# Adding two rope products on VectorE instead of GpSimd, with one of them in the projection's bank, and loading the attention result behind most of the last transposes

## The chip, the cores and the metric

The kernel runs on one core of a Trainium2 chip. The metric is device time in microseconds (us) of one execution. The median of three runs before the change is 1959.97 us.

## What is computed

One transformer layer over 2048 tokens of width 512, in float32: layer norm, RMS norm with a weight, attention with 32 query heads in 8 groups (4 query heads share one key and one value head of 64), rotary embedding of queries and keys, causal softmax, output projection and residual; then layer norm and a feed-forward part with ternary weights.

```python
y = rms_norm(layernorm(x)) * rms_w
y = einsum('bsm,cm->bsc', y, w_in)            # q: 32*64, k: 8*64, v: 8*64
q, k = rope(q), rope(k)                       # x1*cos - x2*sin, x2*cos + x1*sin
attn = softmax(where(causal, q @ k.T / 8, -inf))
x = x + layernorm(x) + (attn @ v) @ w_out.T
x = x + down(silu(up(layernorm(x))) * gate(layernorm(x)))
```

## The kernel before

Every product is kept at more than 16 bits by splitting a number into a high and a low half: high*high, high*low and low*high are added up in PSUM. Three blocks follow one another: `normalise`, `attention` and `output_projection` with the feed-forward part. The change lies in `attention`.

`attention` runs over 8 groups. A group has 16 units, one for each of 4 chunks of 512 queries and each of 4 heads, and a unit goes over the keys up to its chunk in tiles of 128: in all 160 steps, numbered through the group. In a step TensorE makes the scores of one key tile for 512 queries (L598, L599, and L602 on the diagonal), ScalarE takes the exponential (L666), GpSimd subtracts the high half from it, which leaves the low half `pl` (L827, "low part"), and five steps later TensorE multiplies exponentials and values (L615 to L619, "the values of a step"). Those wait for the exponential and for the low part.

Beside the steps runs side work, placed by hand in two tables of step numbers. `JOB_STEPS` gives the steps at which TensorE projects a tile of 128 tokens for the chunks to come (`project`, L567, 12 matmuls): in a middle group steps 0, 4, 10, 16, 26, 27, 42, 53, 88, 101, 118, 123, 141, 146, 151 and 155. `GANG_STEPS` gives the steps at which it makes four score tiles whose maximum per query is wanted (`max_gang`, L583, in two pairs); VectorE reduces them (L742, L746). Projections and these score tiles take turns in four PSUM banks. The bank that an item takes must have been read by the fourth item before it: `side_read` waits for that. For a projection it waits for `v_low`, which the last of four VectorE instructions raises. The gang that follows a projection takes the projection's bank for its fourth tile, in the second pair.

A projected tile goes through `out_of_bank` on VectorE (v's high half, product with the cosines, product of the turned halves with the sines, v's low half). GpSimd adds the two products (`rope_sum`, L833), ScalarE makes high halves of queries and keys (L677 to L680, `qk_high_part`, five steps behind the projection), GpSimd their low halves (L842, `qk_low_part`). The SP queue then turns them by DMA transposes, in the order of the table `TRANSFERS`: q_hh (L448) is wanted by the first gang of a unit, the keys (L465) too, q_lm (L457) by the unit's first scores. The same table turns (L477) and stores (L487) each chunk's result. Every engine executes in program order, so a wait holds up all that stands behind it there.

The opening projects eight tiles before the first group. The last group has no projections ahead (steps 88 to 155 are free of them). In it `load_result` puts four DMAs of 512 KB (L495) into the SP queue, which bring the first two result tiles for the output projection.

Of the kernel before, what the change touches and what calls it, by code (L numbers as in the profile page):

```python
# [11 lines left out]
ALU = mybir.AluOpType  # L12
# [7 lines left out]
TT = S // P  # L20
DH = 64
GROUPS = 8
HG = 4
# [6 lines left out]
NCH = S // CHUNK  # L30
# [186 lines left out]
SUM_LAG = 2  # L217
HI_LAG = 5
QK_LOW_LAG = 4
TILES_KEPT = 4  # L220
# [4 lines left out]
def step_of(i):  # L225
    u = max(w for w in range(UNITS) if FIRST_STEP[w] <= i)
    return u, i - FIRST_STEP[u]
# [121 lines left out]
def slot(part, n):  # L349
    return part[n] if 0 <= n < len(part) else (None, None, [])  # L350
# [7 lines left out]
def attention(nc, w_in_t, w_out_t, attn_dram, yh, yl, consts, cos, sin, wraw, wh, wl, wscale, raw, z_out, late, att_in):  # L358
# [6 lines left out]
    with ExitStack() as ctx:  # L365
        sb = lambda name, shape, dt: ctx.enter_context(nc.sbuf_tensor(name, shape, dt))
        sem = lambda name: ctx.enter_context(nc.semaphore(name))
        ident16, big, mask_kq, mask_qk = (consts[:, i, :] for i in range(4))
        rope_a = sb("rope_a", [P, TILES_KEPT, HG + 1, DH], F32)
        rope_b = sb("rope_b", [P, TILES_KEPT, HG + 1, DH], F32)  # L370
# [4 lines left out]
        v = sb("v", [P, 2, TT, VW], F16)  # L375
# [23 lines left out]
        w_high = sem("w_high")  # L399
        w_low = sem("w_low")  # L400
        misc_ready = sem("misc_ready")
        rope_parts = sem("rope_parts")
        v_high = sem("v_high")
        v_low = sem("v_low")
        roped_ready = sem("roped_ready")
        qk_high = sem("qk_high")
        qk_low = sem("qk_low")
# [30 lines left out]
        def _(sp):  # L438
# [74 lines left out]
            for g in range(GROUPS):  # L513
                final = g == GROUPS - 1
                if not final:
                    sp.wait_ge(w_low, (g + 1) * KT)
                    load_w(g + 1)
                if g == 1:
                    sp.wait_ge(z_out, 16 * NCH)
                sp.wait_ge(exp_done, g * STEPS + EXP_AHEAD)  # L520
                for kind, c, *arg in TRANSFERS:
                    if final and arg[1] == 1:
                        continue
                    {"turn": turn_out, "store": store, "hh": query_high, "lm": query_low, "k": keys}[kind](g, c, *arg)
                    if kind == "store" and 1 <= g <= CT // NCH:
                        load_w_out((g - 1) * NCH + c)
                    if kind == "store" and final and c == 1:
                        load_result()
            sp.wait_ge(w_loaded, 16 * GROUPS)
            sp.wait_ge(w_out_in, 16 * CT)  # L530
# [9 lines left out]
        def _(pe):  # L540
            pe.wait_ge(ones_set, 2)
            def group(g, par, part):
                def side_read(kind, ahead, *arg):

                    if kind == "piece":
                        pe.wait_ge(maxs_used, (g + ahead) * PIECES + FIRST_STEP[arg[0]] + arg[1] + 1)
                    else:
                        pe.wait_ge(v_low, (g + ahead) * TT + arg[0] + 1)

                def take_bank(*item):  # L550

# [168 lines left out]
        def _(dve):  # L720
# [8 lines left out]
            def group(g, par, part):  # L729
# [27 lines left out]
                def out_of_bank(ahead, t):  # L757
                    gg, side, b = g + ahead, par ^ ahead, t % TILES_KEPT
                    bank = side_bank(part, ("proj", ahead, t))
                    halves = bank[:, 0:ROPED].rearrange("p (h a d) -> p h a d", h=HG + 1, a=2)  # L760
                    by_half = lambda a: a.rearrange("p (a d) -> p a d", a=2).unsqueeze(1).broadcast_to([P, HG + 1, 2, DH // 2])
                    roped = lambda a: a[:, b].rearrange("p h (a d) -> p h a d", a=2)
                    dve.wait_ge(misc_ready, gg * TT + t + 1)
                    dve.wait_ge(qk_low, gg * TT + t + 1)
                    nc.vector.tensor_scalar(v[:, side, t, 0:DH], bank[:, ROPED:GC], 1.0 / W_SCALE, None,
                                            ALU.mult).then_inc(v_high, 1)
                    nc.vector.tensor_tensor(roped(rope_a), halves, by_half(cos[:, t, :]), ALU.mult)
                    nc.vector.tensor_tensor(roped(rope_b), halves[:, :, ::-1, :], by_half(sin[:, t, :]), ALU.mult)\
                        .then_inc(rope_parts, 1)
                    dve.wait_ge(v_high, gg * TT + t + 1)  # L770
                    nc.vector.scalar_tensor_tensor(v[:, side, t, VL:VW], bank[:, ROPED:GC], 1.0 / W_SCALE,
                                                   v[:, side, t, 0:DH], ALU.mult, ALU.subtract).then_inc(v_low, 1)

                def unit_out(u):
                    by_tile = obank(u).rearrange("p (t w) -> p t w", w=VU)
# [38 lines left out]
        @block.gpsimd  # L814
        def _(pool):

            nc.gpsimd.memset(qk_lo[:, :, 0:HG, :, 1, :], 0.0).then_inc(rows_set, 1)
            nc.gpsimd.memset(qk_hi[:, :, HG, :, 1, 1:DH], 0.0).then_inc(rows_set, 1)
            nc.gpsimd.memset(qk_hi[:, :, HG, :, 1, 0:1], -1.0).then_inc(rows_set, 1)
            pool.wait_ge(ones_set, 2)  # L820
            def group(g, par, part):
                def low_part(i, ahead=0):
                    u, j = step_of(i)
                    r = first_query_tile(u // HG, j)
                    cols = slice(r * P, CHUNK)
                    pool.wait_ge(exp_done, (g + ahead) * STEPS + i + 1 + EXP_AHEAD)
                    nc.gpsimd.tensor_tensor(pl[:, i % RING, cols], p32[:, i % RING, cols], p_high[:, i % RING, cols],  # L827
                                            ALU.subtract).then_inc(low_ready, 1)

                def rope_sum(ahead, t):  # L830
                    b = t % TILES_KEPT
                    pool.wait_ge(rope_parts, (g + ahead) * TT + t + 1)
                    nc.gpsimd.tensor_tensor(rope_a[:, b], rope_a[:, b], rope_b[:, b], ALU.add).then_inc(roped_ready, 1)  # L833

                def qk_low_part(ahead, t):
                    (c, tt), gg = divmod(t, TPC), g + ahead
                    pool.wait_ge(qk_high, gg * TT + t + 1)
                    if tt == 0 and (ahead or c >= 2):
                        for h in range(HG):
                            pool.wait_ge(lm_in[c % 2][h], 16 * (2 * gg + c // 2))  # L840
                        pool.wait_ge(k_in[(c - 2) % NCH], 32 * (gg + (c >= 2)))
                    nc.gpsimd.tensor_tensor(qk_lo[:, c % 2, :, tt, 0, :], rope_a[:, t % TILES_KEPT], qk_hi[:, c % 2, :, tt, 0, :],  # L842
                                            ALU.subtract).then_inc(qk_low, 1)

                for n in range(len(part) + 2):
                    step = slot(part, n - 1)[0]
                    if step is not None:
                        if step >= HEAD:
                            low_part(step)
                    if job := slot(part, n - QK_LOW_LAG)[1]:  # L850
                        qk_low_part(*job[1:])
                    if job := slot(part, n - SUM_LAG)[1]:
                        rope_sum(*job[1:])
                for i in range(HEAD if part in (OPENING, SLOTS) else 0):
                    low_part(i, ahead=int(part is SLOTS))

            group(0, 0, OPENING)
            every_group(group)
# [507 lines left out]
```

## Time and profile before

| what | value |
|---|---|
| runs, median of 3 (lowest to highest) | 1959.97 us (1959.13 to 1960.13) |
| profiled execution, its own time | 1961.57 us |
| its span | 1959.8 us |
| TensorE busy | 1894.3 us (97%) |
| GpSimd busy | 1421.3 us (73%) |
| VectorE busy | 1220.8 us (62%) |
| ScalarE busy | 932.3 us (48%) |
| attention stage | about 43 to 1444 us of the span |

Busy time is the time in which at least one instruction of the engine ran. Matmuls are pipelined and their ends are modelled, so consecutive ones overlap in the record; what TensorE does is read from the distance between starts. Numbers in the text such as 600.77 are microseconds from the start of the span.

### The profile page before, as it was taken

The numbers are of one execution on the slowest core, as the hardware profiler recorded it, in microseconds if no ns is written. First come the engines' busy times: TensorE is split into PE (matmuls) and PEld (weight loads), VectorE is DVE, ScalarE is ACT, GpSimd is POOL, SyncE is SP. The second block draws the span as 40 slices with busy tenths as digits, with TensorE's granted clock in tenths as the row PEclk, the third lists the DMA queues.
The fourth block names the chain that finished last, engine by engine and source line by source line (L and its number), as shares of the span: only waits on it lengthen the run. The fifth ranks groups of instructions, "written<-read, shape, count | busy, mean of one in ns | idle before, by whom it ended". The sixth has DMA issues, their size and how long they took to land. (4 is left out here: it accounts for less than half of the span.)

```text
span 1959.8 us, 55709 instructions
## 1 busy us (share of the span) xinstructions
PE 1894.3 (97%) x21382; PEld 1093.0 (56%) x21382; DVE 1220.8 (62%) x3283; ACT 932.3 (48%) x1997; POOL 1421.3 (73%) x1627
## 2 busy tenths in 40 slices
PE   4899999999999999999999999998999999999999
PEld 3565666666566666556656665665644444444444
DVE  7787588668758866875886687585726563131221
ACT  4465656556565665655566565555722212120110
POOL 2799989999998999999899999988940002131221
PEclk7999999999999999999999999999999999999999
DMA  6343242333225224332422332144146520000000
GB/s 213 67 68 56 49 97 56 50 83 74 64 50 99 56 47 85 70 69 48 91 50 40 79 63 62 32 90 88 38 154 226 203 86 1 22 0 21 5 16 22
DMA packets 301814, 136.82 MB, mean 70 GB/s; under 512 B 248576, under 2 KB 285696, under 8 KB 300032
## 3 DMA queue, kind: packets, MB, share of 16 engines
q1 hardware_dynamic: 301568, 133.43, 29.7%
q8 instruction: 168, 2.75, 0.6%
q14 instruction: 78, 0.64, 0.1%
HBM read 49.48 MB, written 25.17 MB: 38 GB/s over the span
## 5 line engine op out<-in xcount | busy, mean ns | idle before, releaser
L827 POOL TENSOR_TENSOR pl<-p 128x512 f16<-128x512 f32 (+3 forms) x1280 | 1135.9, 920 | 44.6 <-ACT p L666 44.0
L666 ACT ACTIVATE p<-a_ps 128x512 f32<-128x512 f32 (+3 forms) x1280 | 672.9, 532 | 515.2 <-PE a_ps L599 329.0
L742 DVE TENSOR_REDUCE mpart<-a_ps 128x1 f32<-128x512 f32 x768 | 485.2, 684 | 156.1 <-PE a_ps L583 153.9
L615 PE MATMUL a_ps<-v,p 128*128 128x65 f16 x4352 | 530.4, 194 | 10.9 <-POOL pl L827 5.7
L617 PE MATMUL a_ps<-v,p 128*128 128x64 f16 x4352 | 529.5, 194 | 0.0
L615 PEld LDWEIGHTS a_ps<-v,p 128*128 128x128 bf16 x4352 | 407.2, 97 | 218.5 <-issue 89.3
L619 PE MATMUL a_ps<-v,pl 128*128 128x65 f16 x4352 | 526.2, 192 | 0.0
L599 PE MATMUL a_ps<-q_lm,k_h 128*128 128x512 f16 (+3 forms) x1280 | 445.0, 348 | 0.0
L598 PE MATMUL a_ps<-q_hh,k_hl 128*128 128x512 f16 (+3 forms) x1280 | 444.2, 347 | 0.0
L617 PEld LDWEIGHTS a_ps<-v,p 128*128 128x128 bf16 x4352 | 406.7, 98 | 64.1 <-issue 0.3
L619 PEld LDWEIGHTS a_ps<-v,pl 128*128 128x128 f16 x4352 | 407.6, 99 | 0.0
L746 DVE CUSTOM_DVE_ANT_0 masked<-a_ps,causal 128x128 bf16<-128x128 f32 (+3 forms) x512 | 228.4, 485 | 45.4 <-PE a_ps L583 45.3
L991 POOL TENSOR_TENSOR yl<-o_turn_late,yh 128x512 f16<-128x512 f32 x64 | 74.3, 1163 | 231.1 <-DVE yh L962 231.1
L902 PE MATMUL p_ps<-xh,tern 128*128 (+1 forms) x512 | 194.0, 379 | 0.0
L902 PE MATMUL p_ps<-xl,tern 128*128 (+1 forms) x512 | 194.0, 379 | 0.0
L583 PE MATMUL a_ps<-k_h,q_hh 64*128 64x512 f16 (+2 forms) x640 | 173.0, 339 | 16.5 <-DMA q_hh<-qk_hi 7.9
L583 PE MATMUL a_ps<-k_hl,q_hh 64*128 64x512 f16 (+1 forms) x640 | 187.7, 362 | 0.0
L567 PE MATMUL a_ps<-wh,yh 128*128 128x384 f16 x512 | 168.5, 329 | 8.3 <-DVE v L725 6.8
L567 PE MATMUL a_ps<-wl,yh 128*128 128x384 f16 x512 | 168.1, 328 | 0.0
L567 PE MATMUL a_ps<-wh,yl 128*128 128x384 f16 x512 | 168.1, 328 | 0.0
L942 ACT ACTIVATE p_below<-p_ps,tern_scale 128x512 f32<-128x512 f32 x64 | 43.9, 687 | 249.7 <-PE p_ps L902 249.7
L1130 PE MATMUL p_ps<-yl,yh 128*128 128x512 f16 x480 | 145.6, 379 | 0.0
(103 smaller groups left out, 2373.1 us busy)
## 6 DMA issues: line engine op xcount, KB each, us to landing
yh<-attn_scratch SPq DMA_DIRECT2D x32, 512.0 KB, 4.3
raw<-ffn_t SPq DMA_DIRECT2D x12, 1024.0 KB, 5.0
attn_scratch<-o_turn SPq DMA_DIRECT2D x32, 256.0 KB, 3.1
attn_scratch<-o_turn_late SPq DMA_DIRECT2D x32, 256.0 KB, 2.8
wraw<-w_in_t SPq DMA_DIRECT2D x8, 768.0 KB, 4.8
resid_scratch<-raw SPq DMA_DIRECT2D x4, 1024.0 KB, 4.5
raw<-w_out_t SPq DMA_DIRECT2D x16, 256.0 KB, 3.5
x<-resid_scratch SPq DMA_DIRECT2D x4, 1024.0 KB, 7.8
```

The lines of the kernel that those rows point to most:

```text
L567: last = nc.tensor.matmul(bank[:, 0:GC], a[:, kt, tok], b[:, kt, :], start=(kt == 0 and n == 0), stop=(kt == KT - 1 and n == 2))
L583: nc.tensor.matmul(banks[n % 2][:, 0:width], q_hh[rows, c % 2, h, t * P:(t + 1) * P], keys[rows, par ^ ahead, kk * CHUNK:kk * CHUNK + widt ...
L598: nc.tensor.matmul(out, k_hl[:, side, keys], q_hh[:, c % 2, h, r * P:CHUNK], start=True, stop=False)
L599: last = nc.tensor.matmul(out, k_h1[:, side, keys], q_lm[:, c % 2, h, r * P:CHUNK], start=False, stop=not diag)
L615: nc.tensor.matmul(o, weights, v[:, par, j, 0:VU], start=(j == 0 and t == 0), stop=False, skip_group_check=True)
L617: nc.tensor.matmul(o[:, 0:DH], weights, v[:, par, j, VL:VW], start=False, stop=False, skip_group_check=True)
L619: last = nc.tensor.matmul(o, pl[:, i % RING, t * P:(t + 1) * P], v[:, par, j, 0:VU], start=False, stop=(j == TPC * c + t), skip_group_chec ...
L666: nc.scalar.activation(p32[:, i % RING, r * P:CHUNK], sbank(i)[:, r * P:CHUNK], ACT.Exp, scale=SCALE).then_inc(exp_done, 1)
L742: nc.vector.reduce_max(mpart[:, u % 2, t, kk:kk + 1], bank, AX.X).then_inc(maxs_used, 1)
L746: nc.vector.tensor_tensor_reduce(masked[:, n % 2, 0:width], bank, causal[:, CHUNK - width:CHUNK], 1.0, -LEAST, ALU.add, ALU.max, mpart[:, ...
L827: nc.gpsimd.tensor_tensor(pl[:, i % RING, cols], p32[:, i % RING, cols], p_high[:, i % RING, cols], ALU.subtract).then_inc(low_ready, 1)
L902: last = nc.tensor.matmul(bank, w[:, k, e * P:(e + 1) * P], x[:, k, bass.ds(c * CHUNK, CHUNK)], start=(k == 0 and x is xh), stop=(k == KT ...
```

## The change

The add of the two rope products moves from GpSimd to VectorE. So that VectorE reads one operand from PSUM, the product with the cosines is written over the projection in its bank, after the turned product has been read out of it; the new semaphore `rope_turned` keeps these two apart. The semaphore `v_low` goes, and the bank is now released by `roped_ready`, raised by the add. `load_result` moves in the order of the last group's transfers from behind the store of chunk 1 to behind the q_lm of chunk 3, head 2 (unit 14).

```diff
-                    if kind == "store" and final and c == 1:
+                    if final and (kind, c, arg[0]) == ("lm", NCH - 1, HG - 2):
                         load_result()
...
-                        pe.wait_ge(v_low, (g + ahead) * TT + arg[0] + 1)
+                        pe.wait_ge(roped_ready, (g + ahead) * TT + arg[0] + 1)
...
                     nc.vector.tensor_scalar(v[:, side, t, 0:DH], bank[:, ROPED:GC], 1.0 / W_SCALE, None,
                                             ALU.mult).then_inc(v_high, 1)
-                    nc.vector.tensor_tensor(roped(rope_a), halves, by_half(cos[:, t, :]), ALU.mult)
                     nc.vector.tensor_tensor(roped(rope_b), halves[:, :, ::-1, :], by_half(sin[:, t, :]), ALU.mult)\
-                        .then_inc(rope_parts, 1)
+                        .then_inc(rope_turned, 1)
+                    dve.wait_ge(rope_turned, gg * TT + t + 1)
+                    nc.vector.tensor_tensor(halves, halves, by_half(cos[:, t, :]), ALU.mult).then_inc(rope_parts, 1)
                     dve.wait_ge(v_high, gg * TT + t + 1)
                     nc.vector.scalar_tensor_tensor(v[:, side, t, VL:VW], bank[:, ROPED:GC], 1.0 / W_SCALE,
-                                                   v[:, side, t, 0:DH], ALU.mult, ALU.subtract).then_inc(v_low, 1)
+                                                   v[:, side, t, 0:DH], ALU.mult, ALU.subtract)
+                    dve.wait_ge(rope_parts, gg * TT + t + 1)
+                    nc.vector.tensor_tensor(roped(rope_a), halves, roped(rope_b), ALU.add).then_inc(roped_ready, 1)
...
-                def rope_sum(ahead, t):
-                    b = t % TILES_KEPT
-                    pool.wait_ge(rope_parts, (g + ahead) * TT + t + 1)
-                    nc.gpsimd.tensor_tensor(rope_a[:, b], rope_a[:, b], rope_b[:, b], ALU.add).then_inc(roped_ready, 1)
-
...
-                    if job := slot(part, n - SUM_LAG)[1]:
-                        rope_sum(*job[1:])
```

VectorE's rows for one tile of a middle group, before (the bank is `a_ps`):

```order
L765 TENSOR_SCALAR v<-a_ps 128x64 [waits qk_low,misc_ready]
L767 TENSOR_TENSOR rope_a<-a_ps,cos_sb 128x320
L768 TENSOR_TENSOR rope_b<-a_ps,sin_sb 128x320
L771 SCALAR_TENSOR_TENSOR v<-a_ps,v 128x64 [waits v_high]
L742 TENSOR_REDUCE mpart<-a_ps 128x1 [waits maxs_ready] x2
```

And at the same place of the change:

```order
L765 TENSOR_SCALAR v<-a_ps 128x64 [waits qk_low,misc_ready]
L767 TENSOR_TENSOR rope_b<-a_ps,sin_sb 128x320
L770 TENSOR_TENSOR a_ps<-a_ps,cos_sb 128x320 [waits rope_turned]
L772 SCALAR_TENSOR_TENSOR v<-a_ps,v 128x64 [waits v_high]
L775 TENSOR_TENSOR rope_a<-a_ps,rope_b 128x320 [waits rope_parts]
```

The products have changed places, a wait on VectorE's own result stands before each of the last two operations that need one, and the add follows v's low half.

The SP queue in the last group, behind the store of chunk 1 (- before, + the change):

```order
+L448 DMA_TRANSPOSE q_hh<-qk_hi 128x4x128
+L457 DMA_TRANSPOSE q_lm<-qk_lo 128x4x128
+L448 DMA_TRANSPOSE q_hh<-qk_hi 128x4x128
+L457 DMA_TRANSPOSE q_lm<-qk_lo 128x4x128
+L448 DMA_TRANSPOSE q_hh<-qk_hi 128x4x128
+L457 DMA_TRANSPOSE q_lm<-qk_lo 128x4x128
+L477 DMA_TRANSPOSE o_turn<-o_hl 128x8x128 x2
+L487 DMA attn_scratch<-o_turn 128x4x256 x2
+L448 DMA_TRANSPOSE q_hh<-qk_hi 128x4x128
+L457 DMA_TRANSPOSE q_lm<-qk_lo 128x4x128
 L495 DMA yh<-attn_scratch 128x2048 x4
```

The load (L495) now has ten more entries of the queue ahead of it; one q_lm, that of the last unit, stays behind it.

## Rows read from the trace of the kernel before

**Rows 1.** Windows: one middle group; busy us and instructions of each engine, clock, DMA.

```profile
587.60:759.60 172.00, 170.12 (x2368) 105.36 (x2368) 126.20 (x356) 102.40 (x229) 166.19 (x193) 1.00 0.35 68
```

**Rows 2.** Groups by line and shape, count | busy us, mean ns | idle before.

```profile
L833 POOL TENSOR_TENSOR rope_a<-rope_a,rope_b 128x320 f32<-128x320 f32 x128 | 110.8, 866 | 16.8 <-DVE rope_b L768 16.8
...
L768 DVE TENSOR_TENSOR rope_b<-a_ps,sin_sb 128x320 f32<-128x320 f32 x114 | 54.9, 481 | 0.0
...
L779 DVE TENSOR_TENSOR a_ps<-a_ps,rden 128x256 f32<-128x256 f32 x123 | 53.2, 433 | 4.2
...
L732 DVE SCALAR_TENSOR_TENSOR wl<-wraw,wscale,wh 128x384 f16<-128x384 f32 x28 | 32.5, 1161 | 0.0
...
L787 DVE TENSOR_TENSOR o_hl<-a_ps,o_hl 128x256 f16<-128x256 f32 x60 | 25.0, 416 | 2.0 <-ACT o_hl L695 2.0
```

**Rows 3.** Timeline of VectorE, tile of step 10: start us, us, instruction.

```profile
598.77 0.17 DVE L777 RECIPROCAL rden<-a_ps 128x4 f32<-128x4 f32 x1
598.98 0.43 DVE L779 TENSOR_TENSOR a_ps<-a_ps,rden 128x256 f32<-128x256 f32 x1
599.48 0.22 DVE L765 TENSOR_SCALAR v<-a_ps 128x64 f16<-128x64 f32 x1
599.62 0.48 DVE L767 TENSOR_TENSOR rope_a<-a_ps,cos_sb 128x320 f32<-128x320 f32 x1
600.02 0.48 DVE L768 TENSOR_TENSOR rope_b<-a_ps,sin_sb 128x320 f32<-128x320 f32 x1
600.41 0.21 DVE L771 SCALAR_TENSOR_TENSOR v<-a_ps,v 128x64 f16<-128x64 f32 x1
```

**Rows 4.** Timeline of TensorE, second pair of step 12: [idle before <-releaser].

```profile
600.77 0.21 PE L583 MATMUL a_ps<-k_h,q_hh 64*128 64x128 f16 x1 [0.18 <-DVE v L771]
```

**Rows 5.** Timelines of VectorE and TensorE, tile of step 88.

```profile
682.04 0.21 DVE L771 SCALAR_TENSOR_TENSOR v<-a_ps,v 128x64 f16<-128x64 f32 x1
...
682.45 0.38 PE L583 MATMUL a_ps<-k_h,q_hh 64*128 64x512 f16 x1
```

**Rows 6.** Timeline of TensorE at a group's end.

```profile
757.74 0.22 PE L602 MATMUL a_ps<-consts 128*128 128x128 f16 x1
758.14 0.19 PE L615 MATMUL a_ps<-v,p 128*128 128x65 f16 x1 [0.18 <-POOL pl L827]
...
759.19 0.22 PE L602 MATMUL a_ps<-consts 128*128 128x128 f16 x1
759.82 0.19 PE L615 MATMUL a_ps<-v,p 128*128 128x65 f16 x1 [0.41 <-POOL pl L827]
```

**Rows 7.** Timeline of GpSimd at the same end.

```profile
756.34 0.86 POOL L833 TENSOR_TENSOR rope_a<-rope_a,rope_b 128x320 f32<-128x320 f32 x1
```

**Rows 8.** Timelines of ScalarE and GpSimd behind the tile of step 53.

```profile
651.74 0.24 ACT L680 ACTIVATE qk_lo<-rope_a 128x64 f16<-128x64 f32 x1
...
652.25 0.80 POOL L842 TENSOR_TENSOR qk_lo<-rope_a,qk_hi 128x320 f16<-128x320 f32 x1
```

**Rows 9.** Last group: timelines of SP, TensorE, GpSimd; windows; landing times of L448.

```profile
1354.90 1.68 SPq L448 DMA_TRANSPOSE q_hh<-qk_hi  x1
...
1402.98 19.77 SPq L457 DMA_TRANSPOSE q_lm<-qk_lo  x2
...
1363.53 0.61 PE L583 MATMUL a_ps<-k_h,q_hh 64*128 64x512 f16 x1 [6.77 <-DMA q_hh<-qk_hi]
...
1349.38 11.75 POOL L827 TENSOR_TENSOR pl<-p 128x512 f16<-128x512 f32 x13
...
1373.71 68.62 POOL L827 TENSOR_TENSOR pl<-p 128x512 f16<-128x512 f32 x75 [0.40 <-ACT p L666]
...
1364.00:1366.00 2.00, 2.00 (x19) 0.95 (x16) 1.82 (x4) 0.00 (x0) 0.00 (x0) 0.50 0.00 0
...
DMA to landing us min/median/max: 2.4/2.5/8.6
```

More of the change, by code:

```diff
@@ L401, in attention @@
         misc_ready = sem("misc_ready")
+        rope_turned = sem("rope_turned")
         rope_parts = sem("rope_parts")
         v_high = sem("v_high")
-        v_low = sem("v_low")
         roped_ready = sem("roped_ready")
```

## The prediction

> **What bounds the kernel now.** I take the windows of one middle group first [rows 1]. In 172.0 us TensorE is busy 170.1, GpSimd 166.2, VectorE 126.2 and ScalarE 102.4. Two engines look full. GpSimd's 166 us are honest: its operations follow one another. TensorE's are too many, since a matmul's shown end lies behind the start of the next, so what TensorE really waits for has to be read from the distance of starts. Seven groups of this kind and a shorter last one make the attention stage, so a tenth of a microsecond at one step of a group is worth 0.7 to 0.8 us.
>
> Next come the operations of the change by shape [rows 2]: the rope add costs GpSimd 0.866 us (0.82 from its start to the next one's, since neighbours overlap a little). VectorE's product over 320 columns takes 0.481, one over 256 columns from PSUM to PSUM 0.433 and from PSUM to SBUF 0.416.
>
> Then the timeline of VectorE at one token tile, the third of the group (step 10) [rows 3], and of TensorE behind it [rows 4]. VectorE begins at 599.48 and ends with v's low half at 600.41 + 0.21 = 600.62. The four scoring matmuls of step 12 come next on TensorE. Their second pair, which takes the projection's bank, starts at 600.77, released by that very instruction. So here the bank's release is already what TensorE waits for, and 0.15 us pass from VectorE's end to the matmul.
>
> Last, two places where GpSimd holds TensorE up. At the group's end the values of steps 157 and 159 start 0.40 and 0.63 us behind the matmul before them, where 0.05 to 0.06 is usual (a 128-column matmul at 2.4 GHz): 0.34 + 0.57 = 0.9 us of standstill, both released by GpSimd [rows 6]. And in the last group TensorE stands 6.77 us for a transpose of queries [rows 9].
>
> **The change, part by part.**
>
> *VectorE.* Five instructions in place of four. From the start of v's high half to the bank's release it is now 600.62 - 599.48 = 1.14 us. In the new order the turned product starts at 0.14 and ends at 0.62. The product with the cosines waits for it. Such a wait on the engine's own result is in the trace: the reciprocal ends at 598.77 + 0.17 = 598.94 and the instruction that waits for it starts at 598.98, 0.04 later [rows 3]; without a wait the next starts 0.08 before the end. So the product starts at 0.66 instead of 0.54. It writes into PSUM, which costs 0.01 to 0.02 more over 256 columns [rows 2]; v's low half follows at 1.07, and the add at 1.20, when the product has been ready since 1.16. The add over 320 columns, one operand in PSUM, is like the product (0.48): end at 1.68. The bank is released 0.53 us later, and VectorE is occupied 0.53 us longer (0.40 for the add, 0.12 for the broken overlap, 0.01 for PSUM). Call it x. Neither end is certain, for no in-place product over 320 columns and no such add is in the trace: below, x = 0.41 if the own wait costs nothing (add and PSUM alone); above, 0.65, if both own waits cost what the first does. I take 0.53, by the rows of the same shapes.
>
> The Trainium skill, "VectorE: DVE Perf Modes", section Terms, says that a flush is emitted after every VectorE operation and the next can't issue until the pipe is empty. By that rule operations never overlap, the wait on rope_turned costs nothing, x would be 0.41 and the sum below 1957.5 us. The trace does not show it so: rope_b starts 0.08 us before rope_a ends [rows 3].
>
> Where does x reach TensorE? At steps 4, 10 and 16 the gang of four two slots later has its second pair waiting for the bank, and VectorE has next to no idle time between; three times 0.53 = 1.6 us. That VectorE is pushed as far behind does not add to it, for TensorE comes as late. At step 88 TensorE takes the bank at 682.45, v's low half having ended at 682.04 + 0.21 = 682.25 [rows 5]: of 0.53 only 0.05 is hidden, 0.5 us. At the tiles of steps 27, 42, 53, 101 and 146 the bank is taken 0.3 to 0.6 us after its release, less the 0.15 that passes anyhow; there 0.05 to 0.2 each comes through, 0.6 together (my estimate, in the manner of rows 5). The other six have over 0.8 us. Loss of a group: 1.6 + 0.5 + 0.6 = 2.7 us.
>
> *GpSimd.* 16 adds of 0.82 us go from each group, 13 us of its 166. They count only where TensorE stands for GpSimd. At the group's end GpSimd's chain is the add at 756.34 [rows 7], the low parts of steps 157 and 158, the part qk_lo of the tile, and the low part of step 159. Without this add and the one at step 153, the low parts of 157 and 159 come some 1.5 us earlier, more than the 0.34 and 0.57 us that TensorE stands: all 0.9 us is gained. (The part qk_lo reads a copy by ScalarE that waits for the same add, and moves up with it.) Behind the tiles of steps 26 and 27 a standstill of 0.2 us goes. The third place is steps 65 to 78, where GpSimd runs without a pause since step 55 and TensorE loses 1.3 us. There an add and the 0.82 us of it go, but the part qk_lo that follows at 652.25 reads what ScalarE writes until 651.74 + 0.24 = 651.98, and ScalarE's place for it is between the exponentials of steps 57 and 58 [rows 8]. So GpSimd would reach it 0.6 to 0.8 us early and wait: 0.2 is left, and this tile's gang comes 0.26 later through VectorE. I count nothing. Gain of a group: 0.9 + 0.2 = 1.1 us.
>
> Net: 2.7 - 1.1 = 1.6 us lost in each of seven groups, 11.2 us. The last group has no tiles at steps 88 to 155 and ends behind GpSimd anyway: 1.6 + 0.4 - 0.2 = 1.8 us lost. The opening has nothing of the end of a group; what it loses (its first pieces take the last tile's bank) stands in place of group 0's step 4.
>
> *The load.* Four transfers of 512 KB leave the SP queue ahead of q_hh for unit 12. That transpose was issued at 1354.90, and TensorE resumed at 1363.53: it is the slowest of the line, 8.6 us to land where 2.5 is the median [rows 9]. Moved behind the q_lm of unit 14, the load passes four q_hh, four q_lm, the turn and the store of chunk 2. The stall of 6.77 us goes, and the granted clock of 0.50 (1.2 GHz) that follows it with it. But TensorE is not what ends this group: from 1373.71 GpSimd works 68.62 us without a pause, to the stage's last values. Before that it stood from 1349.38 + 11.75 = 1361.13 on, save for steps 79 to 84, six low parts (three of 512 columns, one each of 384, 256 and 128) that are 4.7 us of work back to back. It can start these at 1361.1, so it ends 1373.71 - 1361.13 - 4.7 = 7.9 us earlier; TensorE is then ahead of it by some 2 us and stays so. The last two q_lm, issued at 1402.98 and 18.6 us later [rows 9], move up with it: the load is issued near 1396 and there some 9 us after (as q_hh was, queued behind it), 30 us ahead of its use and 8 ahead of the last q_lm. Gain 7.9 us; bounds 7.0 (if part of TensorE's lead is lost) and 9.0 (if TensorE's whole loss counted: 6.8, and half of some 5 us at the lower clock).
>
> **Sum.** 11.2 + 1.8 - 7.9 = 5.1 us more. The profiled execution took 1961.57 us (span 1959.8 and 1.8 around it) and is 1.6 above the median of 1959.97; it would be 1966.7, and the median **1965.1 us**.
>
> **Rivals.**
> - *VectorE's part is cheaper* (x of 0.40 to 0.47). For: 57 us of result hang on each microsecond of x, and the own wait rests on one kind of row. At x = 0.41 a group loses 1.7 - 1.1 = 0.6 us: 4.2 + 1.2 - 7.9 = -2.5, 1957.5 us.
> - *GpSimd's relief is worth all it seems to be.* For: it is 97% busy. If steps 65 to 78 also give 0.8 us, a group loses 0.8: 5.6 + 1.0 - 7.9 = -1.3, 1958.7 us. Against: ScalarE's place in rows 8.
> - *The bank's later release reaches TensorE nowhere* (faster). If x stays under 0.36, so that little comes through at steps 4 to 16, the result passes below -3.9; were it wholly hidden, each group would gain 1.1: -7.7 - 0.2 - 7.9 = -15.8, 1944 us. Against: the release named in rows 4.
> - *The add collides with GpSimd.* wl<-wraw, which reads SBUF alone, takes 1.161 us for 384 columns [rows 2]. If the add did likewise, x would be about 1.1, a group lose 5 us more than it gains, and the result be 1990 us. Against: half of its input is in PSUM, like that of o_hl<-a_ps,o_hl at 0.416.
> - *The load finds another victim.* If the last q_lm landed as late as q_hh does now, TensorE would stand some 6 us: 1971. Against: 8 us of distance.
>
> **How the numbers follow.** Chances: the forecast with x of 0.48 to 0.60, 0.50; cheaper VectorE, 0.22; full relief of GpSimd, 0.08; hidden release, 0.09; collision, 0.05; load, 0.06. 0.2%, 3.9 us, is about what the measurement can tell from no change. Slower by more: most of the forecast's half, the collision and the load, 0.56. Within: the cheaper VectorE, full relief and the forecast's lower edge, 0.31. Faster: 0.13. Range 1956 to 1972: x from 0.40 to 0.65 at a gain of 7.9, widened by the bounds of that gain. The likeliest case alone spans 1962 to 1969.
>
> **What would show it.** Right: the bank's instructions take 1.68 us from v's start to the add's end; at step 12 the second pair starts 0.5 us later against the tile; a middle group lasts 173.6 us; ScalarE no longer waits for rope_a while qk_lo on GpSimd now waits for ScalarE; no TensorE wait over 1 us behind q_hh in the last group; GpSimd without a pause to its end. Wrong: a group of 172 us or less (x mis-sized, or GpSimd the true limit), or a new stall of TensorE near 1405 to 1415.

## The result, and the profile after

The changed kernel takes 1967.00 us (median of 6 runs, 1965.28 to 1968.59), the kernel before 1960.14 us beside it (6 runs, 1959.13 to 1962.50). The ratio is 1.0033 with a 95% interval from 1.0021 to 1.0045: the change costs 0.33%, 6.9 us, where 5.1 were forecast. All ratios here are of fast runs; of the last experiment one run of 2719 us, and one of 4834 us of the kernel before beside it, are left out as slow. The profiled execution took 1965.28 us, span 1963.5.

The windows of two middle groups, in the columns of [rows 1]:

```profile
592.35:766.05 173.70, 170.70 (x2373) 106.05 (x2370) 133.56 (x372) 102.22 (x229) 154.10 (x176) 1.00 0.36 67
766.05:939.70 173.65, 170.66 (x2374) 106.01 (x2371) 133.57 (x372) 102.26 (x229) 154.15 (x177) 1.00 0.35 67
```

A group is 1.65 us longer than the 172.0 of [rows 1], though GpSimd has 12 us less to do in it; VectorE has 7.4 more. A group's length is taken here, and in all that follows, from start to start of GpSimd's low part of step 0; "the usual group" is the commonest length in a trace (in most traces one to three of the six middle groups are 0.2 to 0.9 us longer, by a single late moment at changing places, often a transpose of queries that lands late).

The new VectorE groups by line and shape (count | busy us, mean ns | idle before):

```profile
L770 DVE TENSOR_TENSOR a_ps<-a_ps,cos_sb 128x320 f32<-128x320 f32 x114 | 56.9, 499 | 3.9
L775 DVE TENSOR_TENSOR rope_a<-a_ps,rope_b 128x320 f32<-128x320 f32 x114 | 55.4, 486 | 0.0
```

Both are what [rows 2] let one expect: 0.018 us more for a result in PSUM, and an add at the price of a product. The timeline of VectorE at the tile of step 10, and under it that of TensorE at step 12, which answer to [rows 3, 4]:

```profile
604.80 0.23 DVE L765 TENSOR_SCALAR v<-a_ps 128x64 f16<-128x64 f32 x1
604.95 0.48 DVE L767 TENSOR_TENSOR rope_b<-a_ps,sin_sb 128x320 f32<-128x320 f32 x1
605.46 0.50 DVE L770 TENSOR_TENSOR a_ps<-a_ps,cos_sb 128x320 f32<-128x320 f32 x1
605.87 0.21 DVE L772 SCALAR_TENSOR_TENSOR v<-a_ps,v 128x64 f16<-128x64 f32 x1
606.00 0.48 DVE L775 TENSOR_TENSOR rope_a<-a_ps,rope_b 128x320 f32<-128x320 f32 x1
```

```profile
605.53 0.39 PE L583 MATMUL a_ps<-k_h,q_hh 64*128 64x512 f16 x1
...
606.63 0.21 PE L583 MATMUL a_ps<-k_h,q_hh 64*128 64x128 f16 x1 [0.71 <-DVE rope_a L775]
```

From v's start to the bank's release pass 606.00 + 0.48 - 604.80 = 1.68 us, 0.53 more than before. The second pair is released by the add and has stood 0.71 us, where [rows 4] had 0.18: the whole 0.53 reaches TensorE. The waits of TensorE over the middle groups, kernel before and then the changed one (waited for: us in total, times, longest us):

```profile
PE a_ps L615 <- POOL pl L827: 3.1, 10, 0.4
...
PE a_ps L583 <- DVE v L771: 0.9, 5, 0.2
```

```profile
PE a_ps L583 <- DVE rope_a L775: 9.3, 20, 0.7
...
PE a_ps L615 <- POOL pl L830: 0.3, 1, 0.3
```

In five groups the wait for the bank has grown from 0.9 to 9.3 us, the wait for GpSimd has gone from 3.1 to 0.3. The view names only idle time in the record; a standstill hidden by the overlap of matmuls isn't in it. So I also took TensorE's standstills from the distance of starts (start of a matmul less the start of the one before it, less the latter's columns at 2.4 GHz), for group 3 (the groups are counted from 0; this is the one in [rows 1]), by the step at which they lie. Places that differ between before and after, in us:

```
place (tile whose bank)     before  after   | place (behind GpSimd)  before  after
step 6   (tile of step 4)    0.26    0.79   | step 0                  0.39    0.00
step 12  (10)                0.44    0.97   | step 2                  0.56    0.00
step 18  (16)                0.09    0.58   | step 40                 0.20    0.00
step 90  (88)                0.09    0.58   | step 70                 0.28    0.11
steps 30, 45, 55, 103, 149   0.45    1.17   |
steps 20, 33                 0.72    0.85   |
```

The left half is the loss, 2.04 + 0.72 + 0.13 = 2.9 us; the right half is the gain, 0.39 + 0.56 + 0.20 + 0.17 = 1.3. The standstills of [rows 6] are those at steps 0 and 2 by this count.

The last group, by the timeline of GpSimd and that of the SP queue:

```profile
1353.53 0.80 POOL L840 TENSOR_TENSOR qk_lo<-rope_a,qk_hi 128x320 f16<-128x320 f32 x1 [0.40 <-ACT qk_lo L680]
1354.28 92.75 POOL L830 TENSOR_TENSOR pl<-p 128x384 f16<-128x384 f32 x103
```

```profile
1365.33 1.27 SPq L448 DMA_TRANSPOSE q_hh<-qk_hi  x1
...
1406.53 2.09 SPq L457 DMA_TRANSPOSE q_lm<-qk_lo  x1
1408.71 1.95 SPq L495 DMA_DIRECT2D yh<-attn_scratch  x4
```

GpSimd now works without a pause from 1354.28 to the end of the stage, 1447.03, where in [rows 9] it stood for 12 us less six low parts. The q_hh of unit 12 (issued 1365.33) lands after 3.0 us, against 8.6; the longest landing of the line from 1340 on is 3.7. The load stands far behind. No wait of TensorE from 1340 to the end of the stage exceeds 0.5 us. The group takes 160.1 us against 166.0.

From the trace: the last group starts 10.6 us later than before, is 5.9 shorter, the stage ends 4.7 later, and the span is 3.7 longer. The medians differ by 6.9, since the profiled execution of before lies 1.4 us above its median and that of the changed kernel 1.7 below its own. Two microseconds are no more than single executions scatter.

### The profile page after: what moved, and what is told of

The parts are those of the page before. It is cut to its first block and busy times, and to the rows that moved or that the text cites. A ratio compares the mean times of both kernels' runs of the same rounds, so it can differ in the third digit from the quotient of the medians.

```text
span 1963.5 us, 55709 instructions
## 1 busy us (share of the span) xinstructions
PE 1895.3 (97%) x21382; PEld 1095.8 (56%) x21382; DVE 1280.2 (65%) x3411; ACT 930.8 (47%) x1997; POOL 1323.6 (67%) x1499
## 5 line engine op out<-in xcount | busy, mean ns | idle before, releaser
L583 PE MATMUL a_ps<-k_h,q_hh 64*128 64x512 f16 (+2 forms) x640 | 180.0, 339 | 24.1 <-DVE rope_a L775 15.4
L583 PE MATMUL a_ps<-k_hl,q_hh 64*128 64x512 f16 (+1 forms) x640 | 195.1, 363 | 0.0
L840 POOL TENSOR_TENSOR qk_lo<-rope_a,qk_hi 128x320 f16<-128x320 f32 x128 | 102.0, 797 | 74.9 <-ACT qk_lo L680 70.0
```

The lines of the kernel that those rows point to most:

```text
L583: nc.tensor.matmul(banks[n % 2][:, 0:width], q_hh[rows, c % 2, h, t * P:(t + 1) * P], keys[rows, par ^ ahead, kk * CHUNK:kk * CHUNK + widt ...
```

## The experiments

In the first four the kernel before ran beside them in 1959.55 us (median of 9 runs).

**The load alone** (kernel before with the new place of the load).

```diff
-                    if kind == "store" and final and c == 1:
+                    if final and (kind, c, arg[0]) == ("lm", NCH - 1, HG - 2):
```

> The kernel before with the load of the result tiles moved alone; the rope add stays on GpSimd. My theory: the stall of 6.8 us goes and GpSimd ends the stage 7.9 us earlier, so the time is 8 us under the kernel before (7 to 9), with middle groups of 172.0 us. Rival (the load finds another victim, or the stall was hidden anyway): within 3 us of before, and a wait of some microseconds behind q_lm near 1405 to 1420.

Measured: 1952.59 us, ratio 0.9963 (0.9950 to 0.9977), 7.0 us less. The last group takes 158.05 us instead of 166.02, so 8.0 us, and GpSimd's timeline shows the same single stretch as above:

```profile
1341.46 0.79 POOL L842 TENSOR_TENSOR qk_lo<-rope_a,qk_hi 128x320 f16<-128x320 f32 x1
1342.21 92.65 POOL L827 TENSOR_TENSOR pl<-p 128x384 f16<-128x384 f32 x103
```

The 92.65 us are the length of this chain, whoever feeds it. The load was worth what GpSimd's pause was worth.

The 8.0 us are those of one execution. The stall of TensorE behind q_hh, 6.77 us in [rows 9], differs from trace to trace: over the eight traces here that have the load at its old place it is 4.3 to 6.9 us, 5.6 in the mean, though the order of the transfers is the same in all. So the profiled execution of the kernel before lies near the upper end. With the mean stall the load would be worth about 6.8 us, which is 8.0 less the 1.2 us by which 6.77 lies above 5.6 (an estimate); the medians show 7.0.

**The add alone** (the change, with the load where it was).

```diff
-                    if final and (kind, c, arg[0]) == ("lm", NCH - 1, HG - 2):
+                    if kind == "store" and final and c == 1:
```

> The change with the load left at its old place. My theory: middle groups of 173.6 us, the old stall of 6.8 us is back, and the time is 13 to 15 us over the kernel before. Rival (the add costs less and the moved load did harm): 5 to 9 us over before.

Measured: 1974.79 us, ratio 1.0076 (1.0062 to 1.0089), 15.2 us more; the usual middle group 173.7 us, as in the whole change. The two parts add up to 8.2 us, against 6.9 measured for both: no interplay that these intervals could show. The interval of the 15.2 is wide, 12 to 17 us.

**No add at all** (kernel before, `rope_sum` without its add).

```diff
                     nc.vector.tensor_tensor(roped(rope_b), halves[:, :, ::-1, :], by_half(sin[:, t, :]), ALU.mult)\
-                        .then_inc(rope_parts, 1)
+                        .then_inc(roped_ready, 1)
...
-                    if job := slot(part, n - SUM_LAG)[1]:
-                        rope_sum(*job[1:])
```

> The kernel before with the rope add left out altogether: queries and keys are made of the product with the cosines alone, and ScalarE waits for the two products. It gives what GpSimd's relief is worth with nothing put on VectorE. My theory: 1.1 us in a middle group (170.9 us) and 8 us in all, since behind the tile of step 53 GpSimd waits for ScalarE's copy instead. Rival (GpSimd is the limit, its relief counts in full): 2 us or more in a group, 16 us or more in all.

Measured: 1951.09 us, ratio 0.9954 (0.9940 to 0.9967), 8.5 us less. The windows of one group:

```profile
584.52:755.25 170.73, 169.60 (x2374) 105.52 (x2371) 125.91 (x356) 102.10 (x229) 154.06 (x177) 1.00 0.37 68
```

GpSimd loses 12.1 us of work in the group, and the group 1.3. This is the ceiling of what the change could ever give through GpSimd. In the waits from 110 to 1268 us GpSimd now stands 45.8 us for ScalarE's copy ahead of qk_lo, where it stood 4.1 us before:

```profile
POOL qk_lo L842 <- ACT qk_lo L680: 45.8, 74, 1.3
```

**The add on VectorE for two tiles only** (those of steps 151 and 155, with the load moved).

```diff
+ON_VECTOR = ((1, 6), (1, 7))
...
-                    if kind == "store" and final and c == 1:
+                    if final and (kind, c, arg[0]) == ("lm", NCH - 1, HG - 2):
...
-                        pe.wait_ge(v_low, (g + ahead) * TT + arg[0] + 1)
+                        pe.wait_ge(roped_ready if (ahead, arg[0]) in ON_VECTOR else v_low, (g + ahead) * TT + arg[0] + 1)
```

> The kernel before with the load moved, and with the add on VectorE for two of a group's sixteen tiles only, those of steps 151 and 155, whose banks are taken over 0.8 us after their release. My theory: all of the 0.9 us at a group's end is gained and no bank is waited for: middle groups of 171.1 us, the time 14 us under before (12 to 15). Rival (the end of a group gives little, what counts is the load): as with the load alone, 8 us under before.

Measured: 1946.19 us, ratio 0.9930 (0.9917 to 0.9944), 13.4 us less. The usual group takes 171.07 us, 0.93 less than in [rows 1]: two adds of sixteen bring three quarters of the 1.3 us. (The lines above leave out that VectorE adds for these two tiles as in the change, that `rope_sum` passes them over, and that each engine waits for the sum of the tile before, so that `roped_ready` counts in order.) With the load's 7.0 that leaves 13.5 us, and 13.4 came.

**A filler on VectorE, ahead of or behind v's low half** (on the kernel before, which took 1959.82 us beside the first pair and 1960.41 beside the second).

```diff
+        spare = sb("spare", [P, TILES_KEPT, 480], mybir.dt.uint8)
...
                         .then_inc(rope_parts, 1)
+                    nc.vector.memset(spare[:, b, :], 0)
                     dve.wait_ge(v_high, gg * TT + t + 1)
```

> The kernel before, with the load and GpSimd's add as they were, and one memset more on VectorE at every tile (480 elements of one byte, meant to last about 0.5 us), between the rope product and v's low half. The projection's bank comes free 0.5 us later, as in the change, while GpSimd gets nothing off. Theory (the loss is that of the bank's release and of VectorE's time, 2.7 us a group, with 1.1 us of relief against it in the change): middle group 174.7 to 174.9 us, total about 21 us above before. Rival (the loss is the new waits of VectorE on its own results or a collision of its add with GpSimd, both absent here): a group within 0.5 us of 172.1, no more than 4 us above before.

```diff
                                                    v[:, side, t, 0:DH], ALU.mult, ALU.subtract).then_inc(v_low, 1)
+                    nc.vector.memset(spare[:, b, :], 0)
```

> The same memset of the same length, but behind v's low half: the bank comes free when it does in the kernel before, and only VectorE is busy longer. Theory (most of the loss is the bank's): a loss only where VectorE has no idle time behind the tile, steps 4 to 22 and 27, about 1.3 us a group, 10 us in all. Rival (VectorE's busy time alone counts): as late as the run with the memset ahead of v's low half, about 21 us. Rival (only the bank counts): within 3 us of before.

Measured: 1960.64 us (1.0005, 0.9996 to 1.0014) and 1960.27 us (1.0001, 0.9992 to 1.0010). By the numbers expected this is the rival's result. But the profile shows that the dose was never given:

```profile
L771 DVE MEMSET spare<- 128x120 uint32 x114 | 18.0, 158 | 0.0
```

480 bytes were written as 120 words in 0.158 us, and v's low half behind it took 161 ns instead of 215: the bank came free 1.23 us after v's start, 0.08 late. With the memset behind v's low half VectorE was occupied 0.13 us longer. The pair says only that so little costs next to nothing. It was run again with words of four bytes:

```diff
+        spare = sb("spare", [P, 664], F32)
...
+                    if gg * TT + t:
+                        dve.wait_ge(v_low, gg * TT + t)
+                    nc.vector.memset(spare[:, :], 0)
                     dve.wait_ge(v_high, gg * TT + t + 1)
```

> As the run with a memset between the rope product and v's low half, but with 664 elements of four bytes: that run's 480 bytes were written as 120 words in 0.158 us, so that the bank was released only 0.08 us later than before (1.230 against 1.152 us from v's start). By the four sizes of memset in the traces (0.085 us for 32 elements, 0.158 for 120, 0.165 for 128, 0.218 for 192) this one takes 0.61 us and releases the bank 0.53 us late, as the change does. A wait for the v_low of the tile before is added, long fulfilled. Load and GpSimd's add as in the kernel before. Theory (bank's release and VectorE's time cost 2.7 us a group): middle group 174.8 us, 21 us above before. Rival (neither matters; the loss lies in VectorE's waits on its own results or in its add beside GpSimd): under 172.8 us, within 5 us of before.

```diff
+        spare = sb("spare", [P, 1, 600], F32)
...
                                                    v[:, side, t, 0:DH], ALU.mult, ALU.subtract).then_inc(v_low, 1)
+                    nc.vector.memset(spare[:, 0, :], 0)
```

> A memset of 600 elements of four bytes behind v's low half: the bank is released in time (1.15 us from v's start) and VectorE is busy until 1.68 us, as in the change. Theory (mostly the bank): 0.5 to 1.5 us a group, 4 to 11 us above before. Rival (VectorE's busy time alone counts): as much as the run that also releases late. Rival (only the release counts): within 2 us of before.

Measured: late release 1985.58 us (1.0131, 1.0116 to 1.0147), 25 us more where 21 were expected; bank in time 1970.16 us (1.0053, 1.0039 to 1.0067), 9.8 us more where 4 to 11 were expected. In both the theory fits. The first one's timeline on VectorE at the tile of step 10, and its waits on TensorE:

```profile
610.49 0.22 DVE L766 TENSOR_SCALAR v<-a_ps 128x64 f16<-128x64 f32 x1
...
611.60 0.61 DVE L773 MEMSET spare<- 128x664 f32 x1
612.13 0.16 DVE L775 SCALAR_TENSOR_TENSOR v<-a_ps,v 128x64 f16<-128x64 f32 x1
```

```profile
604.97 0.21 PE L584 MATMUL a_ps<-k_h,q_hh 64*128 64x128 f16 x1 [0.64 <-DVE v L775]
612.44 0.21 PE L584 MATMUL a_ps<-k_h,q_hh 64*128 64x128 f16 x1 [0.82 <-DVE v L775]
```

This dose came out too large: the release is 1.80 us after v's start, 0.65 late, for the memset starts 0.09 us behind the product's end, where the short one had started 0.03 ahead of it. The usual group took 175.3 us, 3.3 more than before, without any add on VectorE and without a wait for the result just made. So a late bank and a longer occupied VectorE make such a loss by themselves.

The same trace shows that loss and gain are not separate terms. At the places behind GpSimd TensorE stands less here too, though GpSimd keeps all its adds: by the distance of starts 0.20 us less at step 40, 0.19 at step 70 and 0.24 at step 0, which fits that TensorE comes later there. The places at the banks lose 3.9 us, and 3.3 are left.

In the second the bank is in time and VectorE is occupied 0.63 us longer, a little more than the 0.53 meant. The usual group takes 173.4 us, 1.4 more. TensorE stands elsewhere, behind the reductions of the maxima (TensorE's timeline, start, us, [idle before]):

```profile
615.79 0.37 PE L584 MATMUL a_ps<-k_h,q_hh 64*128 64x512 f16 x1 [0.52 <-DVE mpart L743]
616.37 0.32 PE L584 MATMUL a_ps<-k_h,q_hh 64*128 64x384 f16 x1 [0.18 <-DVE mpart L747]
```

By the distance of starts the places 6, 12, 18 and 90 are as before here, and 9, 13, 15, 20 and 33 have 1.6 us more together (0.2 behind GpSimd goes at step 40 here as well). In the changed kernel, and in the run with the late bank, those places are within 0.1 us of before: there TensorE comes as late as VectorE. The two losses are alternatives and not a sum. With a bank released in time the loss would shrink, but not go: 1.4 us of a group stay in this run, in which GpSimd keeps its adds.

**The add from SBUF** (both products to SBUF as before, the add behind v's low half on VectorE).

```diff
+                    dve.wait_ge(rope_parts, gg * TT + t + 1)
+                    nc.vector.tensor_tensor(rope_a[:, b], rope_a[:, b], rope_b[:, b], ALU.add).then_inc(roped_ready, 1)
```

> The add goes to VectorE, the load stays, but both products go to SBUF as before and the add reads SBUF alone, behind v's low half: the bank comes free as in the kernel before. Theory (bank's release matters most, collision is mild): the bank's part of the loss is gone, VectorE's time costs about 1.3 us a group, GpSimd's relief gives 1.1 back: within 4 us of before, 0 to 6 above; the add itself 0.5 us. Rival (collision: two operands in SBUF hold GpSimd's operations up, or are held up by them): the add about 1 us, GpSimd's low parts beside it longer, a middle group of 175 us or more, over 20 us above before.

Measured: 1977.54 us, ratio 1.0090 (1.0076 to 1.0104), 17.7 us more, a group of 174.5 us: the rival, nearly in full. The add by line and shape, then two of its executions in the timelines of VectorE and of GpSimd:

```profile
L774 DVE TENSOR_TENSOR rope_a<-rope_a,rope_b 128x320 f32<-128x320 f32 x114 | 91.0, 798 | 0.0
```

```profile
442.69 0.48 DVE L774 TENSOR_TENSOR rope_a<-rope_a,rope_b 128x320 f32<-128x320 f32 x1
...
574.54 3.08 DVE L774 TENSOR_TENSOR rope_a<-rope_a,rope_b 128x320 f32<-128x320 f32 x1
```

```profile
442.72 2.34 POOL L829 TENSOR_TENSOR pl<-p 128x512 f16<-128x512 f32 x2 [1.29 <-ACT p L666]
...
572.51 4.76 POOL L829 TENSOR_TENSOR pl<-p 128x512 f16<-128x512 f32 x6
```

The mean of 0.80 us hides several kinds. 95 of the 128 adds take 0.48 us, 20 take 0.7 to 1.1, and 13 take 2.5 to 3.1. At 442.69 the add starts just ahead of two low parts, and these take 2.34 us where two take 2.04 elsewhere. At 574.54 it starts while GpSimd goes from one low part to the next, and is not through before GpSimd's row ends at 572.51 + 4.76 = 577.27: it ends at 577.62, and all of VectorE's work behind it is late. The add of the changed kernel, with one operand in PSUM and beside the same low parts, is never held: 119 of its 128 executions overlap an instruction of GpSimd, and the longest takes 0.488 us. Nor does it hold GpSimd up. Of the 896 low parts of 512 columns, 28 take over 1.15 us in the kernel before and 28 in the changed one, each time beside wl<-wraw; with the add from SBUF it is 102. That operand is what the in-place product buys.

VectorE's longer occupation alone does not explain this run. The filler behind the release occupied VectorE longer (0.63 us against 0.40 here), with nothing taken off GpSimd, and cost 9.8 us.

The Trainium skill, "SBUF — State Buffer", section "SBUF: two separate sides", says that a VectorE operation with two SBUF inputs and a GpSimd operation that reads SBUF exclude one another for a whole instruction, whichever starts first. The run agrees in that one is held while the other runs (0.48 us become 3.08, a low part of 1.04 becomes 1.34), and shows in addition that the add let four GpSimd operations pass.

**The change with two VectorE instructions exchanged** (turned product first, then v's high half).

```diff
+                    nc.vector.tensor_tensor(roped(rope_b), halves[:, :, ::-1, :], by_half(sin[:, t, :]), ALU.mult)\
+                        .then_inc(rope_turned, 1)
                     nc.vector.tensor_scalar(v[:, side, t, 0:DH], bank[:, ROPED:GC], 1.0 / W_SCALE, None,
                                             ALU.mult).then_inc(v_high, 1)
-                    nc.vector.tensor_tensor(roped(rope_b), halves[:, :, ::-1, :], by_half(sin[:, t, :]), ALU.mult)\
-                        .then_inc(rope_turned, 1)
                     dve.wait_ge(rope_turned, gg * TT + t + 1)
```

> The change with two VectorE instructions exchanged: the turned product first, then v's high half, then the product with the cosines, whose wait for the turned product is then fulfilled when it comes. By the starts in the trace of the change the bank is released some 0.10 us earlier (1.57 to 1.59 us from the first start, against 1.68). Theory (5 us of a group hang on a microsecond of this time): middle group 173.1 to 173.2 us, total 3.5 to 4.5 us below the change, about 3 us above before. Rival (the loss is not in the time of release): as the change, 1967 us.

Measured: 1957.81 us, ratio to before 0.9986 (0.9977 to 0.9995), 9 us below the change by the two ratios (6.8 us by the spans of the two profiled executions). The timeline of VectorE at a tile, and a window of one group:

```profile
602.10 0.49 DVE L765 TENSOR_TENSOR rope_b<-a_ps,sin_sb 128x320 f32<-128x320 f32 x1
602.51 0.22 DVE L767 TENSOR_SCALAR v<-a_ps 128x64 f16<-128x64 f32 x1
602.64 0.49 DVE L770 TENSOR_TENSOR a_ps<-a_ps,cos_sb 128x320 f32<-128x320 f32 x1
603.04 0.21 DVE L772 SCALAR_TENSOR_TENSOR v<-a_ps,v 128x64 f16<-128x64 f32 x1
603.17 0.49 DVE L775 TENSOR_TENSOR rope_a<-a_ps,rope_b 128x320 f32<-128x320 f32 x1
```

```profile
589.77:762.40 172.63, 170.27 (x2374) 105.99 (x2370) 132.05 (x372) 102.24 (x229) 154.06 (x177) 1.00 0.36 68
```

The product with the cosines starts 0.08 us before its neighbour ends, and the tile takes 1.56 us instead of 1.68. These 0.13 us take 1.0 us from a group, twice what I had expected: I had reckoned with 5 us of a group for each microsecond of release, while the four full and the five partial places each give back nearly all of it, about 8. (The prediction has that rate in its rival of a cheaper VectorE: 1.0 us for 0.12. My expectation for this run did not use it.) By the rule of the Trainium skill that the prediction weighed ("VectorE: DVE Perf Modes", section Terms) this exchange would have been worth nothing; the measurement says otherwise.

**Eleven tiles on VectorE** (exchanged order; all tiles but those of steps 0, 4, 10, 16 and 88; load moved; 1958.92 us beside it, median of 10 runs).

The table, against that of the run with two tiles (the lines leave out the exchange of the two instructions):

```diff
-ON_VECTOR = ((1, 6), (1, 7))
+ON_VECTOR = tuple((0, t) for t in range(12, 16)) + tuple((1, t) for t in range(1, 8))
```

> The load behind the last q_lm, the add on VectorE for the eleven tiles of a group at whose bank the trace of the change loses little (steps 26, 27, 42, 53, 101, 118, 123, 141, 146, 151, 155), in the exchanged order that releases it at 1.55 us; on GpSimd, as before, for the five others (0, 4, 10, 16, 88). Theory (each place has its own margin, and GpSimd's relief counts at three places): relief of 1.2 us a group as in the run without the add, less 0.06 at step 33 and 0.13 at step 55, the two places where the exchanged order still held TensorE: middle group 171.1 us, and 171.3 with two tiles; in all about 1.5 us below the run with two tiles, near 1945. Rival (VectorE's occupancy over more tiles, or the hand-over of the sum between two engines, costs elsewhere): a group over 171.5 us and over 1947.

Measured: 1944.85 us (median of 5 runs), ratio 0.9928 (0.9915 to 0.9941); the usual group 170.90 us, with two tiles 171.07. Of 0.2 us that were expected, 0.17 came in these groups: the waits at steps 40 and 70 went, and 0.06 and 0.12 us came back at steps 33 and 55. But three of the six middle groups are 0.5 to 0.7 us longer, two of them by a wait for q_hh, and over all six the mean is 171.2 us against 171.3. In the medians the two kernels can't be told apart. Both beat the kernel before by 0.7%.

## Why the prediction was right

- **x, the later release.** Forecast 0.53 us, measured 0.53 (1.681 against 1.152 in the median over 128 tiles). Its parts held too: add 0.486, PSUM 0.018 more, and the broken overlap, which the exchanged order gave back. The own wait behind the product does cost: the next instruction starts 0.035 us behind the end (0.04 forecast from the one row in [rows 3]) and not 0.083 before it. The prediction's 57 us of result for each microsecond of x is not quite what its own rival gives, 7.6 us for 0.12, or 63.
- **Where x reaches TensorE.** Forecast 1.6 + 0.5 + 0.6 = 2.7 us a group, measured 2.04 at the four full places and 0.72 at five partial ones, and 0.13 at steps 20 and 33, which I had not counted. In all the loss was forecast 0.2 us too low. The run with the late bank alone shows that release and occupancy suffice.
- **That VectorE being pushed adds nothing.** Right as a statement on the sum. But the filler behind the release shows 1.4 us a group that stand in for the bank's loss when the bank is in time; the prediction had no number for that.
- **GpSimd's relief.** Forecast 1.1 us, measured 1.3, and the same 1.3 with no add at all. The group's end gave 0.95 (0.9 forecast), confirmed by the two tiles alone (0.93), and the place behind steps 26 and 27 0.2. Steps 65 to 78, counted at nothing, gave 0.17. By the run with the late bank, the 0.37 us at steps 40 and 70 go without any relief of GpSimd once TensorE is late; without an add and without lateness they go too. So in the changed kernel they can't be put down to the relief alone. The reason given for the small gain at steps 65 to 78 holds, for there GpSimd now waits for ScalarE:

```profile
658.52 0.24 ACT L680 ACTIVATE qk_lo<-rope_a 128x64 f16<-128x64 f32 x1
```

```profile
657.39 1.04 POOL L830 TENSOR_TENSOR pl<-p 128x512 f16<-128x512 f32 x1 [0.41 <-ACT p L666]
658.84 0.80 POOL L840 TENSOR_TENSOR qk_lo<-rope_a,qk_hi 128x320 f16<-128x320 f32 x1 [0.40 <-ACT qk_lo L680]
```

- **Net of a group.** Forecast 173.6 us, measured 173.65. That it fits so well is in part luck: loss and gain were each forecast 0.2 us too low, and the two cancel.
- **The load.** Forecast 7.9 us (7.0 to 9.0): 8.0 in the last group of the one trace, 7.0 in the medians. The size rested on one execution whose stall was near the upper end of what the traces show (4.3 to 6.9 us). What it was worth was GpSimd's pause; TensorE's own 6.8 us and its lower clock were not to be added.
- **The sum.** Forecast 5.1 us, 4.7 at the end of the attention stage, 6.9 in the medians. The parts measured singly were 15.2 for the add (13.0 forecast) and 7.0 for the load. So by the medians the load's term is 0.9 us too large and the add's 2 us too small, though its groups agree to 0.1 us. Both forecasts lie inside the intervals (load 4.5 to 9.8 us, add 12 to 17), so no run shows either miss to be more than scatter.
- **The rivals.** A cheaper VectorE: x was not 0.41 here; the exchanged order brought it to 0.40, and a group then lost 0.6 us, as that rival reckoned. Collision: not in the change (28 slow low parts before and after), but nearly in full once both operands lay in SBUF. Hidden release, GpSimd's full relief (1.3 us is the whole) and another victim of the load did not occur.

## What to carry to other kernels

Ask of work taken off a busy engine at which places another engine stands for it: here 2 of 16 adds carried three quarters of the relief, and moving just these was 20 us faster than moving all (11 us faster than moving all in the better order of instructions), by the ratios. Ask the same of the engine that gets the work: what it holds (a bank) comes free later by every instruction put ahead of the release, at each place without a margin. And read a filler's duration in the profile before its time is taken as an answer.

## What the runs showed of the hardware

- An add on VectorE with both operands in SBUF let a whole row of GpSimd operations pass (3.08 us for 0.48 of work, ending 0.35 us after the row); with one operand in PSUM the same add took 0.486 us in the mean and 0.488 at most, beside GpSimd at work.
- A VectorE instruction that waits on a semaphore for the one just before it started 0.03 us behind its end (128 products of the changed kernel), one without such a wait 0.08 before it. With an unrelated instruction in between the wait cost nothing.
- A memset of 480 bytes ran as 120 words in 0.158 us, and started 0.03 us before the end of the instruction ahead of it. One of 664 words of four bytes took 0.61 and started 0.09 behind that end, one of 600 words 0.07 behind, though no wait had been added there. Why was not looked into.
- A DMA transpose issued right behind four DMAs of 512 KB on the same queue landed 7.3 to 8.8 us after its issue in eight traces, where 2.5 us is the median of the line. How long TensorE stood for it varied more, 4.3 to 6.9 us.
